# A one-core block of quantised gated linears and a mixture of experts: a first batch shared out anew between engines, all order lists rewritten, a later load and a reordered tail

## What is computed

```python
def smooth_quant_linear(x, w):          # x [T, D], w [O, D]
    s = sqrt(max(|x| over rows) / max(|w| over rows))        # one per column
    xs, ws = x / s, w * s
    x_scale, w_scale = max|xs| per row / 127, max|ws| per row / 127
    return round(xs / x_scale) @ round(ws / w_scale).T * x_scale * w_scale.T

h = smooth_quant_linear(layernorm(x), fside)         # fside [512, 512] per batch
gate, up = split(h)
x = x + tanh(g_xattn) * smooth_quant_linear(silu(gate) * up, ctx)   # ctx [512, 256]

n = layernorm(x)
top-2 of 16 experts by softmax(n @ gate_w), 256 slots per expert, the rest dropped
expert(t) = (silu(t @ w_gate) * (t @ w_up)) @ w_down          # inner width 352
shared(t) = the same with one pair of weights of inner width 704, for all rows
x = x + tanh(g_ffn) * (weighted expert rows + shared(n))
```

## Time and profile before

| | us |
|---|---|
| median of 3 runs (579.65, 580.83, 579.65) | 579.65 |
| the profiled execution | 581.87 |
| its span, first to last instruction | 579.8 |
| around the span | 2.07 |
| PE busy | 546.2 (94%) |
| DVE, ACT, POOL busy | 419.4, 331.0, 154.3 |
| mean granted clock of PE | 0.985 |

### The profile page before, as it was taken

One profiled execution on the slowest core, in us unless ns is written; L12 is line 12 of the kernel. 1 busy time (PEld: TensorE's weight loads), 2 busy tenths in 40 slices (PEclk: granted clock), 3 DMA queues, 4 the chain that ended last, 5 costly groups with the idle time before them and its releaser, 6 DMA issues.

```text
span 579.8 us, 10175 instructions
## 1 busy us (share of the span) xinstructions
PE 546.2 (94%) x3768; PEld 464.0 (80%) x3776; DVE 419.4 (72%) x828; ACT 331.0 (57%) x570; POOL 154.3 (27%) x187
## 2 busy tenths in 40 slices
PE   7897879999999999999799999999999999999995
PEld 3453548986888788887799999999999999999983
DVE  3778988998899786586376666766676776566766
ACT  3285876686558527522367677766666666742321
POOL 3437780431043010104022211111111100166610
PEclk9988999999999999999899999999999999999998
DMA  7930130014001130115757776666777767457742
GB/s 265 386 131 2 37 136 11 2 37 145 1 5 35 73 101 1 77 46 165 244 165 263 246 252 222 222 222 227 242 244 260 245 218 241 148 167 214 232 147 99
DMA packets 45891, 89.52 MB, mean 154 GB/s; under 512 B 4304, under 2 KB 24784, under 8 KB 44832
## 3 DMA queue, kind: packets, MB, share of 16 engines
q1 hardware_dynamic: 40736, 72.26, 36.7%
q0 software_dynamic: 5120, 16.78, 9.3%
HBM read 72.25 MB, written 16.78 MB: 154 GB/s over the span
## 4 chain that ended last, share of the span: by engine, by line
PE 62%; DVE 19%; ACT 6%; POOL 6%; issue 4%; DMA 2%; another core or an unknown queue 1%; SPq 0%; DVEq 0%; POOLq 0%; ACTq 0%
PE ps_gu L1854 10%; PE ps_gu L1855 10%; PE ps_gu L1856 10%; PE ps_d L1854 6%; PE ps_d L1856 5%; PE ps_d L1855 5%; PE ps_a L2108 3%; PE ps_gu L1896 2%; POOL w L486 2%; DMA raw_d<-in_L_ffn_w_down 2%; PE ps_gu L2415 2%; POOL sw_lo L502 1%; PE ps_d L1875 1%; DVE bn_b L1093 1%; ACT y L754 1%
## 5 line engine op out<-in xcount | busy, mean ns | idle before, releaser
L1854 PE MATMUL ps_gu<-ex_xhi,w_hi 128*128 128x256 f32 x352 | 99.4, 283 | 0.2 <-DVE ex_xlo L1469 0.2
L1855 PE MATMUL ps_gu<-ex_xlo,w_hi 128*128 128x256 f32 x352 | 99.5, 283 | 0.0
L1856 PE MATMUL ps_gu<-ex_xhi,w_lo 128*128 128x256 f32 x352 | 99.4, 282 | 0.0
L1854 PEld LDWEIGHTS ps_gu<-ex_xhi,w_hi 128*128 128x128 f32 x352 | 67.0, 190 | 2.5 <-DVE ex_xlo L1469 0.5
L1855 PEld LDWEIGHTS ps_gu<-ex_xlo,w_hi 128*128 128x128 f32 x352 | 67.1, 191 | 1.8
L1856 PEld LDWEIGHTS ps_gu<-ex_xhi,w_lo 128*128 128x128 f32 x352 | 67.1, 191 | 0.0
L1854 PE MATMUL ps_gu<-xt_hi,sw_hi 128*128 128x256 f32 x220 | 65.1, 296 | 0.1
L996 ACT ACTIVATE ex_hhi<-ex_hid 128x256 fp32r<-128x256 f32 (+1 forms) x66 | 27.5, 417 | 64.6 <-DVE ex_hid L1715 58.0
L1855 PE MATMUL ps_gu<-xt_lo,sw_hi 128*128 128x256 f32 x220 | 62.0, 282 | 0.0
L1856 PE MATMUL ps_gu<-xt_hi,sw_lo 128*128 128x256 f32 x220 | 62.0, 282 | 0.0
L1854 PE MATMUL ps_d<-wd_hi,ex_hhi 128*128 128x512 f32 x132 | 54.3, 411 | 6.6 <-DVE ex_hlo L1717 6.5
(11 more groups left out here) (255 smaller groups left out, 1411.4 us busy)
## 6 DMA issues: line engine op xcount, KB each, us to landing
raw_gu<-in_L_ffn_w_gate SPq DMA_DIRECT2D x16, 704.0 KB
raw_gu<-in_L_ffn_w_up SPq DMA_DIRECT2D x16, 704.0 KB
raw_d<-in_L_ffn_w_down SPq DMA_DIRECT2D x16, 512.0 KB
expert_out_scratch<-eo SPq DMA_DIRECT2D x16, 512.0 KB
w<-in_fside_BxS2xS SPq DMA_DIRECT2D x4, 1024.0 KB, 5.4
x2n_scratch<-y SPq DMA_DIRECT2D x4, 1024.0 KB, 3.9
x<-in_x SPq DMA_DIRECT2D x1, 3072.0 KB, 16.5
raw_d<-in_L_ffn_w_down SPq DMA_DIRECT2D x16, 192.0 KB
```

The source lines that it names most:

```text
L1854: pe.matmul(dst, a_hi, b_hi, start=start, stop=False)
L1855: pe.matmul(dst, a_hi, b_lo, start=False, stop=False)
L1856: return pe.matmul(dst, a_lo, b_hi, start=False, stop=stop)
```

## The change

It has five parts; the kernel's arithmetic result is meant to be the same.

1. **First batch.** `normalise_a(0)` and `normalise_b(0)` move from ACT to DVE, as four `tensor_scalar` instructions each; ACT keeps them for the other batches. Of the four tiles of `quant_w(0)` ACT keeps two (`quant_w_first`), DVE gets two (`quant_w_rest`), and `turn_qw(0)` waits for both. `silu_a(0)` and `gate_up(0)` go in two halves (`silu_half`, `gate_up_half`). `split_gu_lo`, `split_d_lo` and `norm_a` are moved on POOL, `router` on ACT and DVE later, and the counts in `keep_busy` are changed.
2. **Lists.** The lists of PE, DVE and ACT for batches 1 to 3 and the shared expert are written in another order, with the same calls. At their end `sum_shared(1, 1)` stands ahead of `top_two(3)`.
3. **Down weights last.** SP loads expert 1's gate and up weights, waits until they are there, and only then starts the load of its down weights. ACT's `weights_gu(1)` waits for the former alone. `weights_d(0, 0)` comes after `tokens(0, 0)`.
4. **Packed chunk second.** In the last half of the tail the packed chunk of 96 is the second and the full one the third (`part_at`), and the last product signals after its first half of the rows.
5. **Rows added ahead.** In the tail DVE's `add_rows(2, ...)` and `add_last(...)` come one chunk earlier.

```diff
 
+    def part_at(e, m):
+
+        return (0, 2, 1)[m] if e == NE - 1 else m
...
             load_w2(3)
-            store_x2n(2)
             sp.wait_ge(gated_done, B)
             load_gu(0, wg_v[0], wu_v[0])
+            store_x2n(2)
             store_x2n(3)
             sp.wait_ge(x2n_out, 16 * B)
             sp.wait_ge(full_b, unit_b(B - 1, B_X2T + C - 1) + 1)
             sp.wait_ge(raw_in[0], 32)
             load_d(0, w_down[0])
             sp.wait_ge(sh_gu, CHUNKS)
-            load_raw(1, 1)
+            load_gu(1, wg_v[1], wu_v[1])
+            sp.wait_ge(raw_in[1], 32)
+            load_d(1, w_down[1])
 
             def split_done(e):
...
             norm_a(0)
             root_a(0)
             scale_w(0)
-            split_gu_lo(0)
             norm_a(1)
-            split_gu_lo(1)
-            norm_a(2)
+            split_d_lo(0)
             root_b(0)
             scale_w2(0)
             root_a(1)
+            split_gu_lo(0)
+            scale_w(1)
+            split_gu_lo(1)
+            norm_b(0)
             split_gu_lo(2)
-            scale_w(1)
-            split_d_lo(0)
-            norm_b(0)
+            split_gu_lo(3)
             split_d_lo(1)
-            split_gu_lo(3)
...
 
+            def quant_w_first(a):
+
+                act.wait_ge(w_steps_done[LA], a + 1)
+                    last = act.activation(w1[:, j, :], w1[:, j, :], ACT.Copy, bias=MAGIC + LOW16, scale=small[LA]["w_inv"][:, j:j + 1])
+                last.then_inc(qw_done[LA], 1)
+
...
+            def silu_half(a, h):
+
+                t = slice(HALF * h, HALF * h + HALF)
+                for j in range(HALF * h, HALF * h + HALF):
+                    emptied_a(act, unit_a(a, A_H + j))
+                act.activation(gated[:, t, :], xn[:, t, 0:I2], ACT.Silu).then_inc(silu_done if h else silu_first_done, 1)
...
-                act.wait_ge(raw_in[q], 32 if isinstance(e, int) and e == 0 else 64 * k + 64)
...
             def weights_d(e, q):
+                if isinstance(e, int) and e < 2:
+                    act.wait_ge(raw_in[q], 64)
                 if isinstance(e, int) and e == 0:
-                    act.wait_ge(raw_in[q], 64)
...
-            normalise_a(0)
             tanh()
             copy_s(0)
             quant_x(0)
             ints_x(0, 0)
-            quant_w(0)
+            quant_w_first(0)
             ints_x(0, 1)
             copy_w(0)
             ints_w(0, 0)
             ints_w(0, 1)
             split_gu_hi(0)
+            split_d_hi(0)
+            silu_half(0, 0)
             split_gu_hi(1)
-            router()
-            split_d_hi(0)
-            silu_a(0)
+            silu_half(0, 1)
             abs_w(1)
             normalise_a(1)
             abs_x(1)
...
                 hidden(e, e % 2, 0, False)
-                hidden(e, e % 2, 1, False)
+                hidden(e, e % 2, 1, False, part_at(e, 1))
                 if e % 2 and t < len(TAIL):
                     tokens(E + t, t % 2)
-                hidden(e, e % 2, 2, False)
...
+
+            def normalise_a(a):
+
+                dve.wait_ge(rstd_a_done, 4 * a + 4)
+                for j in range(J):
+                    last = dve.tensor_scalar(xn[:, j, :], x2[:, a, j, :], rstd_a[:, a, j:j + 1], shift_a[:, a, j:j + 1], ALU.mult, ALU.add)
...
+
+            def quant_w_rest(a):
+
+                dve.wait_ge(w_steps_done[LA], a + 1)
+                for j in range(HALF, J):
+                    last = dve.tensor_scalar(w1[:, j, :], w1[:, j, :], small[LA]["w_inv"][:, j:j + 1], MAGIC + LOW16, ALU.mult, ALU.add)
...
+
+            def gate_up_half(a, h):
+
+                t = slice(HALF * h, HALF * h + HALF)
+                dve.wait_ge(silu_done if h else silu_first_done, 1)
+                last = dve.tensor_tensor(gated[:, t, :], gated[:, t, :], xn[:, t, I2:D], ALU.mult)
+                if h:
+                    last.then_inc(gated_done, 1)
...
             amax_w(0, 2)
+            normalise_a(0)
...
-            amax_w2(0, 0)
             scale_x(0)
             x_steps(0)
             w_steps(0)
+            quant_w_rest(0)
             stats_a(1)
+            amax_w2(0, 0)
             stats_a(2)
-            amax_w2(0, 1)
             dequant_a(0, 0)
             dequant_a(0, 1)
+            amax_w2(0, 1)
             dequant_a(0, 2)
             dequant_a(0, 3)
-            router()
-            gate_up(0)
+            gate_up_half(0, 0)
+            gate_up_half(0, 1)
+            amax_g(0, 0)
             peaks_w(1)
...
                 b, h = TAIL[t]
-                dve.wait_ge(ex_d, M * NE)
                 dve.wait_ge(sum_last, HALF)
                 for k in range(HALF):
                     j = HALF * h + k
+                    if k == 0:
+                        dve.wait_ge(first_half_done, 1)
+                    else:
+                        dve.wait_ge(ex_d, M * NE)
...
             hidden(E + 4, 0, 0)
             shared_rows(1)
-            hidden(E + 4, 0, 1)
             dve.wait_ge(ex_eo, E + 1)
             add_rows(2, 0)
+            hidden(E + 4, 0, 1)
+            add_rows(2, 1)
             hidden(E + 4, 0, 2)
-            add_rows(2, 1)
-            hidden(E + 5, 1, 0)
             dve.wait_ge(ex_eo, E + 2)
             add_last(0)
+            add_last(1)
+            hidden(E + 5, 1, 0)
+            add_last(2)
             hidden(E + 5, 1, 1)
-            add_last(1)
+            add_last(3)
             hidden(E + 5, 1, 2)
-            add_last(2)
-            add_last(3)
             last_rows()
...
                 pe.wait_ge(qw_done[LA], a + 1)
+                if a == 0:
+                    pe.wait_ge(qw_rest_done, 1)
...
-            def fill_d(q, bank, k, m, first, final):
+            def fill_d(q, bank, k, m, first, final, halves=None):
                 for h in range(HALF):
                     t = slice(h * P, (h + 1) * P)
                     last = three(ps_d[:, 2 * bank + h, :], ex_hhi[0:k, m, t], ex_hlo[0:k, m, t],
                                  wd_hi[q][0:k, m, :], wd_lo[q][0:k, m, :], first, final)
+                    if halves is not None and h == 0:
+                        last.then_inc(halves, 1)
                 last.then_inc(ex_d, 1)
...
-                n, k = M * (E + 2 * t + w) + m, ROWS[m]
+                n, part = M * (E + 2 * t + w) + m, part_at(E + 2 * t + w, m)
...
 
             def tail_down(t, w, m):
 
-                n, k = M * (E + 2 * t + w) + m, ROWS[m]
...
                     pe.wait_ge(ex_eo, E - 1 + t)
                 if m == 0:
```

456 lines of the change are left out of this document (238 added, 218 removed).

## The result

The changed kernel takes 574.18 us in the median (573.06, 574.22, 574.78, 574.14) against 579.65 (578.91 to 580.83): ratio 0.9903, 95% interval 0.9888 to 0.9919. The direction was right, the size was not: less than half of the forecast gain came, and the time lies 0.7 us above the top of the range. A second set of executions of the same kernel gave 573.46 and 0.9904 (0.9880 to 0.9927).

What follows compares the result with a forecast made beforehand. Bound by a chain through all engines in stage A, PE's own work in B and C, the chain behind the last product in the tail. 5.25 + 0.5 + 4.5 + 3.0 = 13.25 us saved: median 566.4, range 562 to 573.5.

Steps and rivals of the forecast that it cites:

- the baseline: Whole kernel: the saving summed on the profiled run (581.87 us) carries over unchanged to the median, 2.2 us lower.
- Stage A: First 92 us, chain through all engines: logits of batch 0 start at about 85.3, not 90.5; gain 5.25, bounds 3.0 and 6.5.
- ratio_b (silu, gate, maxima): First batch: silu and gate product in halves, the first beside waiting; about 2.3 us becomes 1.25, gain 1.05.
- second normalise ends: First batch, `normalise_b` on DVE: starts up to 0.9 later, takes 1.5 to 2.5 for ACT's 2.93; gain 0.55, bounds 1.0 and -0.4.
- logits (x_lo): Behind the second normalise: x_lo splits no longer alternate with four dequants of 0.75 us; gain 0.95, bounds 0 and 1.5.
- rival (3): First batch: DVE and POOL slow each other, late splits and normalises take longer; 2 us lost, time 568.4; chance 0.08.
- Stage B: Same products up to the experts; PE's 0.69 us wait for a shared sum goes; gain 0.5, bounds 1.5 and -1.5.
- Rival (1): 92 to 145 us: batch 1's DVE steps not ready, PE waits; up to 5.25 us given back, time 571.6; chance 0.22.
- Start of the experts: Expert 1's weights start earlier; PE's wait falls from 3.70 to 0.9 us, no clock fall; gain 4.5, bounds 5.4 and 1.8.
- Rival (4): Experts' loop: loads fall behind and PE waits in each of 14 experts; with 2 us each 594 us; chance 0.04.
- Tail: End of program: 7.4 us becomes 4.0, new PE waits cost 1.4, 0.55 and 0.4 come back; gain 3.0, bounds 3.7 and 0.5.
- Rival (2): Tail: ACT's 5.02 us pause, an instruction fetch, comes two chunks later and costs PE about 3 us; time about 569; chance 0.12.

Runs made afterwards that it cites:

- padded kernel before: The kernel before with seven padding matmuls in PE's two waits ahead of the first transpose of y: 579.38 us, ratio 1.0004.
- normalise on ACT: The changed kernel with the second normalise of batch 0 put back from DVE to ACT: 569.9 us, ratio 0.9844; repeated 570.47, 0.9847.
- spread and padded: The changed kernel with batch 0's second normalise on ACT, `split_d_lo(0)` spread over POOL's gaps, 10 padding matmuls in PE's wait: 569.02 us, ratio 0.9832.

## Why the prediction was wrong, step by step

Two baselines are needed: the profiled execution of before, on which my sum stood, and the padded kernel before, which has the time of before's median (span 576.9, about 579.0).

| at | before, profiled | before, padded | after | normalise on ACT | spread and padded |
|---|---|---|---|---|---|
| root_b used | 52.54 | 52.03 | 49.69 | 49.76 | 47.40 |
| second normalise ends | 84.06 | 83.45 | 83.34 | 81.12 | 79.76 |
| logits | 90.52 | 88.40 | 89.53 | 86.07 | 84.71 |
| first expert product | 274.78 | 272.78 | 273.88 | 270.40 | 269.16 |
| tokens of expert 15 | 488.50 | 487.24 | 483.39 | 480.10 | 479.07 |
| span | 579.8 | 576.9 | 571.0 | 567.6 | 566.7 |

**The first step that failed: the baseline.** "The median is 2.2 below that run, and I carry the saving over as it is." That was wrong by 2.9 us. The difference was no constant; it sat in places that the change touches: 2.0 ahead of the experts (1.5 with the clock fallen at 84 to 88 us, the rest there before the fall, 0.5 of it already when root_b is used), -0.7 in the experts, and 1.6 in the tail, where ACT's pause of 5.02 us and the wait of 1.11 behind it are absent in the padded kernel's trace. I took 90.52 as the time of the logits and counted 0.55 for the pause; the median had neither. Against its own profile the changed kernel gains 8.8 of span, against the usual case 5.9, and the medians say 5.5.

**Stage A: forecast 5.25, measured 1.0 against the profile, -1.1 against the usual case.** Term by term, from the kernel before's profile to the changed kernel's:

| up to | before, after | forecast | measured |
|---|---|---|---|
| last column maximum | 17.99, 17.20 | 0.5 | 0.8 |
| first dequant (rounding) | 39.06, 37.15 | 0.9 | 1.1 |
| ratio_b (silu, gate, maxima) | 50.49, 48.88 | 1.05 | -0.3 |
| root_b used | 52.54, 49.69 | 1.0 | 1.25 |
| shift_b (between) | 81.09, 78.09 | 0.3 | 0.15 |
| second normalise ends | 84.06, 83.34 | 0.55 | -2.3 |
| logits (x_lo) | 90.52, 89.53 | 0.95 | 0.3 |

The small steps were real, though the first owes its 0.8 to the baseline: in the padded kernel the last maximum ends at 17.02. Two failed: the gate with the maxima behind it, beside a POOL that I had moved there myself (`gated` 2.90 for 1.4, `abs_a` 2.09 for 1.2), and above all `normalise_b`, sized at 1.5 to 2.5 us and measured at 4.44, outside my bounds. I had named the cause as rival (3) and put 2 us and 0.08 on it; the normalise back on ACT and the split spread over gaps are worth 4.0 us together (569.02 against 572.98, both padded, on one chip), of which about 0.9 is DVE's order behind the normalise. The error was to price a contention by POOL's side alone, its 5.04 against 3.60. DVE's side was in the same trace, and I did not look at it. DVE's rows of the kernel before, with POOL's split of 45.01 to 50.05 beside the first and no split beside the second; the third has POOL's next split beside it:

```profile
47.05 1.30 DVE L1108 TENSOR_TENSOR abs_a<-abs_a 128x512 f32<-128x512 f32 x1
...
54.05 0.69 DVE L1108 TENSOR_TENSOR abs_a<-abs_a 128x512 f32<-128x512 f32 x1
...
73.13 3.11 DVE L1315 TENSOR_TENSOR x<-x,y 128x2048 f32<-128x2048 f32 x1
```

```profile
70.36 8.26 POOL L510 TENSOR_TENSOR sd_lo<-raw_sd,sd_hi 128x512 fp32r<-128x512 f32 x5
```

The same addition takes 2.29 in the three other batches. So the profile that I predicted from showed steps of DVE at 1.4 and 1.9 times their length beside POOL. The x_lo gain of 0.95 shows as 0.3 against the profile, which had the fallen clock there, and is a loss of 1.2 against the usual case (6.19 from the end of the normalise to the logits, 4.95 before), since DVE has one dequant and `abs_b` between the normalise and the low parts (0.9) and the clock fell (0.3). The Trainium skill's rule (page "Advanced Engine Details and Errata", section "Mode Summary", that VectorE's second port is shared with GpSimd and the two hold each other up) is borne out for fp32 `tensor_scalar` (1.88 against 4.44). It names VectorE's two-port modes, in which that section doesn't list `tensor_tensor`; the products of two SBUF sources were held up here as well (0.69 against 1.45 each). The estimate of 1.6 us from the page "VectorE: DVE Perf Modes", section "The perf-mode tier table", came out at 1.88 to 1.91 where POOL was still: nearer to it than to the 2.47 of bn_stats, but 0.3 above.

**Stage B: forecast 0.5, measured 0.** The single wait went, others of 0.5 to 0.8 came, and the length from `shared_up` to the experts is the same to 0.1. Rival (1), 0.22, did not occur in the changed kernel.

**Start of the experts: forecast 4.5, measured 4.95** against the usual case (from 272.78 to 487.24 there, from 273.88 to 483.39 here), 4.2 against the profile. Expert 1's weights were begun at 275.60 (I took 277.2), PE waited 0.23 for 0.9, and the clock stayed at 1.00. Rival (4) did not occur: no wait in the loop from 292 to 540 us.

**Tail: forecast 3.0, measured 2.05** (from the tokens of expert 15 to the end: 89.66 and 87.61). The end itself gives 3.1 for 3.4. The new waits between chunks come to 1.0 for 1.4: in the usual case one chunk follows another at the rate of PE, in the changed kernel each of the last three starts 0.2 to 0.4 later than that. The 0.55 and 0.4 that I counted for the pause and for less work are not there.

**Rival (2), the late silu, 0.12.** The changed kernel's trace has no such pause anywhere, and the padded kernel before has none either. The reading behind the rival was off: in the profile's count 556 instructions of ACT lie ahead of the late silu, not 512. On the two chips named above pauses of 2.7 to 11.8 us end on ACT at places between 512 and 556 us, so at no fixed instruction of its list, in kernels whose ACT list is the same up to there; the fetch at a block's edge (the Trainium skill, "Runtime: NRT & Kernel Launch", "Instruction fetch mechanics") is not supported by this. What causes them stays open. All lie in the time in which POOL issues its gathers of rows (497 to 561 us); whether that is the cause was not tried.

Summed over the usual case: -1.1 + 0 + 4.95 + 2.05 = 5.9 for 13.25. Of the 7.35 missing, 6.35 are stage A, of which about 2 come from the baseline. The range was also drawn narrower than its terms: their poor bounds (3.0, -1.5, 1.8 and 0.5) add up to a gain of 3.8, a time of 575.9, which would have held the 574.18; and their good ones to 16.5, a time of 563.2 and not 562. The version that beats both kernels keeps parts 2 to 5, the first normalise, the rounding and the gate's halves on DVE, leaves the second normalise on ACT, spreads POOL's split over gaps and pads one wait: 569.02, ratio 0.9832.

## What to carry to other kernels

Before a sum is made on one profiled execution that lies above the median, find where the excess is: a fall of the clock behind a wait, or a pause, counts as a gain only if the median has it too. When work moves to VectorE, look at what GpSimd does in the same microseconds, on both sides: a fp32 step from SBUF to SBUF took more than twice its time there (4.44 for 1.88), the same step on ScalarE did not (2.93 both times). And when two chains end a program at nearly the same time, look for both: each alone gave 1.2 to 1.3 us here, the two together 3.1.

## What the runs showed of the hardware

- Four fp32 `TENSOR_SCALAR` of 128x512 on DVE, SBUF to SBUF: 1.88 to 1.91 us alone, 4.44 beside POOL's `TENSOR_TENSOR`; two products of 128x512: 1.37 alone, 2.90 beside it. ACT's four of the same size take 2.93 either way. DVE's steps from PSUM (`dequant_a`, 0.74) keep their time. POOL's eight tiles of 128x352: 7.80 with the normalise on ACT, 8.49 with it on DVE, 9.25 beside DVE's other work; four alone 3.60.
- The granted clock fell to 0.50, for less than 4 us each time, behind a stretch in which PE waited. With waits of 1.39 and 0.41 us it did so in three executions of eight of the same instructions; with waits of 0.60 to 0.81 and 2.13 to 4.06 in all seven traces that have them; with 0.81 and 1.77 in neither of two. Padding in the waits held it at 1.00 in all three kernels that had it. From the end of the normalise to the logits a fall cost 1.5 us where PE set the pace (6.46 against 4.95) and 0.3 where DVE did (6.19 against 5.89).
